# Attention kernel: value products of two steps issued together at every second step, four buffers of exponentials in place of two

## What is computed

```python
B, T, C, H = 8, 1024, 256, 16          # d = C // H = 16
h = layernorm(x) * (1 + ca) + sa
q, k, v = heads(h @ Wq + bq), heads(h @ Wk + bk), heads(h @ Wv + bv)
att = einsum('bhtd,bhsd->bhts', q, k) / sqrt(d)
att = softmax(where(causal, att, -inf), axis=-1)
y = einsum('bhts,bhsd->bhtd', att, v)
x = x + ga * (y.reshape(B, T, C) @ Wp + bp)
```

## Time and profile before

| | us |
|---|---|
| median of 3 runs | 5697.3 |
| lowest and highest run | 5688.06, 5707.4 |
| the profiled execution | 5709.35 |
| span of its profile | 5707.6 |

### The profile page before, as it was taken

One profiled execution on the slowest core, in us unless ns is written; L12 is line 12 of the kernel. 1 busy time (PEld: TensorE's weight loads), 2 busy tenths in 40 slices (PEclk: granted clock), 3 DMA queues, 4 the chain that ended last, 5 costly groups with the idle time before them and its releaser, 6 DMA issues. The chain is left out here.

```text
span 5707.6 us, 95645 instructions
## 1 busy us (share of the span) xinstructions
PE 4571.6 (80%) x31246; PEld 3181.5 (56%) x31246; DVE 3285.3 (58%) x7520; ACT 2605.4 (46%) x5522; POOL 1900.6 (33%) x1482
## 2 busy tenths in 40 slices
PE   2899899899997588887887888848788788787886
PEld 1344444444443466666666666646666666666665
DVE  1555565655553557566575575637557566575564
ACT  0344444444443445455454454535445454454453
POOL 2112212221222334333343343424334343344443
PEclk6787998987887789899899998979899999898988
DMA  5224324423410100000000000020000000000000
GB/s 104 62 42 98 87 42 91 98 42 80 98 31 26 58 16 10 13 13 11 15 12 13 15 10 13 13 59 15 18 21 15 19 17 15 21 15 19 17 17 20
DMA packets 155733, 200.20 MB, mean 35 GB/s; under 512 B 29900, under 2 KB 130728, under 8 KB 155184
## 3 DMA queue, kind: packets, MB, share of 16 engines
q1 hardware_dynamic: 151088, 192.13, 13.8%
q10 hardware_dynamic: 4096, 1.06, 0.1%
HBM read 116.02 MB, written 67.68 MB: 32 GB/s over the span
## 5 line engine op out<-in xcount | busy, mean ns | idle before, releaser
L958 DVE TENSOR_REDUCE a_mx<-a_ring 128x2 f32<-128x1024 f32 (+3 forms) x768 | 728.1, 957 | 439.2 <-PE a_ring L793 293.8
L1477 POOL TENSOR_TENSOR b_e<-b_e,b_share 128x512 f32<-128x512 f32 (+1 forms) x512 | 531.6, 1038 | 1288.6 <-DVE b_share L1905 1288.6
L632 ACT ACTIVATE a_e_t<-a_ring 128x1024 f32<-128x1024 f32 (+3 forms) x768 | 609.3, 810 | 729.0 <-PE a_ring L819 490.2
L1580 ACT ACTIVATE b_e<-b_e,b_bias 128x256 f32<-128x256 f32 (+1 forms) x1024 | 498.7, 488 | 606.5 <-DVE b_bias L1885 605.2
L1683 PE MATMUL b_bank_m<-b_h_t_hi,b_w_hi 128*128 128x256 f32 x1584 | 473.5, 299 | 93.7 <-POOL b_h_t_lo L1483 72.0
L1683 PE MATMUL b_bank_p<-b_wqkv_hi,b_turned_hi 128*128 128x512 f32 x768 | 376.6, 490 | 187.1 <-ACT b_qk L1552 141.2
L788 PE MATMUL a_ring<-a_k_st,a_q_st 48*128 48x512 f32 (+3 forms) x1536 | 370.5, 480 | 125.1 <-ACT a_e_t L632 59.5
L1683 PE MATMUL b_bank_m<-b_h_t_lo,b_w_hi 128*128 128x256 f32 x1584 | 458.9, 290 | 0.0
L1683 PE MATMUL b_bank_m<-b_h_t_hi,b_w_lo 128*128 128x256 f32 x1584 | 458.0, 289 | 0.0
L1885 DVE CUSTOM_DVE_ANT_0 b_e<-b_bank_s,b_mask,b_scale_q 128x256 f32<-128x256 f32 (+1 forms) x1024 | 433.9, 460 | 0.2
L815 PE MATMUL a_ring<-a_q_st,a_k_st 50*128 50x512 f32 (+3 forms) x1536 | 367.1, 475 | 67.6 <-DVE a_qk_p L937 40.3
(11 more groups left out here) (220 smaller groups left out, 11066.7 us busy)
## 6 DMA issues: line engine op xcount, KB each, us to landing
a_q_st<-a_parts_q SPq DMA_DIRECT2D x192, 128.0 KB, 4.4
a_k_st<-a_parts_k SPq DMA_DIRECT2D x192, 128.0 KB, 7.2
b_fl<-f_rows SPq DMA_DIRECT2D x72, 256.0 KB, 4.0
a_parts_q<-a_qk_p SPq DMA_DIRECT2D x16, 1024.0 KB, 9.5
a_parts_k<-a_qk_p SPq DMA_DIRECT2D x16, 1024.0 KB, 4.0
a_xl<-in_L_attn_x SPq DMA_DIRECT2D x9, 1024.0 KB, 9.2
f_rows<-b_fr SPq DMA_DIRECT2D x33, 256.0 KB, 2.3
b_x_l<-x_rows SPq DMA_DIRECT2D x33, 256.0 KB, 3.7
```

Source lines behind the costliest of these rows:

```text
L632: act.activation(e_t[:, step % 2, 2 * pair:2 * pair + 2, 0:cols], slot[:, :].rearrange("p (h t) -> p h t", h=2)[:, :, 0:cols], ACT.Exp).th ...
L958: dve.reduce_max(mx[:, g % 2, :, pair, piece, t:t + 1], slot[:, :].rearrange("p (r c) -> p r c", r=2)[:, :, 0:cols], AX.X)\
L1477: pool.tensor_tensor(weights, weights, share[:, pp, :].unsqueeze(2) .broadcast_to([P, 2, 2 * WIN - lo]), ALU.mult).then_inc(e_done.sem, 1)
L1580: ins = act.activation(weights, weights, ACT.Exp, scale=-1.0, bias=bias[:, pp, hh:hh + 1], accum_out=total[:, pp, hh:hh + 1])
```

## The change

`e_t` gets four buffers (`EBUF = 4`), and ACT waits for the values of four steps before. `meet_values` is no longer called in every step: step n with n even calls it for n - 2 and then n - 1, step 0 for steps 10 and 11 of the group before, and odd steps don't call it. No product, no mask and no reader is added or left out.

```diff
--- before.py
+++ after.py
@@ -221,6 +221,7 @@
 NUNIT = len(UNITS)
 PER_STEP = NUNIT // NSTEP
 UNIT_LEAD = 4
+EBUF = 4
 
 
 def units_at(g, n):
@@ -340,7 +341,7 @@
         q_st = sb("a_q_st", [P, H1 // 2, T], F32R)
         k_st = sb("a_k_st", [P, H1 // 2, T], F32R)
         v_t = sb("a_v_t", [P, TB, H1, VW])
-        e_t = sb("a_e_t", [P, 2, 4, 512])
+        e_t = sb("a_e_t", [P, EBUF, 4, 512])
         w_raw = e_t[:, :, :, :].rearrange("p a b (c n) -> p (a b c) n", n=C)[:, 0:CK * NW, :]\
             .rearrange("p (k w) n -> p k w n", k=CK)
         mx = sb("a_mx", [P, 2, 2, 2, 2, TB])
@@ -627,9 +628,9 @@
                     slot, filled, back, k = slot_of(("s", g, n, pair))
                     act.wait_ge(filled.sem, filled.at(a, k + 1))
                     if pair == 0:
-                        act.wait_ge(values_met.sem, values_met.at(a, step - 1))
+                        act.wait_ge(values_met.sem, values_met.at(a, step - EBUF + 1))
                     cols = 512 * (half + 1) - max(512 * half, P * s)
-                    act.activation(e_t[:, step % 2, 2 * pair:2 * pair + 2, 0:cols],
+                    act.activation(e_t[:, step % EBUF, 2 * pair:2 * pair + 2, 0:cols],
                                    slot[:, :].rearrange("p (h t) -> p h t", h=2)[:, :, 0:cols],
                                    ACT.Exp).then_inc(back.sem, 1)
 
@@ -832,7 +833,7 @@
                         pe.wait_ge(out_read.sem, out_read.at(a, 2 * g + half))
                     for h in range(4):
                         mm = pe.matmul(outp[32 * h:32 * h + VW, lo:512], v_t[:, s, 4 * g + h, :],
-                                       e_t[:, (g * NSTEP + n) % 2, h, 0:512 - lo],
+                                       e_t[:, (g * NSTEP + n) % EBUF, h, 0:512 - lo],
                                        start=(s == 0), stop=(s == 4 * half + 3))
                     mm.then_inc(values_met.sem, 1)
 
@@ -865,9 +866,11 @@
                         scores(g, n, 1, a)
                         for group, k, at in units[1:]:
                             first_pass(group, k, at)
-                        if n > 0:
+                        if n % 2 == 0 and n > 0:
+                            meet_values(g, n - 2, a)
                             meet_values(g, n - 1, a)
-                        elif mode != "lead":
+                        elif n == 0 and mode != "lead":
+                            meet_values((g - 1) % G1, NSTEP - 2, a - (g == 0))
                             meet_values((g - 1) % G1, NSTEP - 1, a - (g == 0))
                         if n == 1 and mode != "lead":
                             turn_output((g - 1) % G1, 1, a - (g == 0), g, a)
@@ -881,6 +884,7 @@
                         if n == 8 and has_maxima(mode, g):
                             turn_maxima(nxt, nxt_a)
                 if mode == "closing":
+                    meet_values(LAST, NSTEP - 2, i)
                     meet_values(LAST, NSTEP - 1, i)
                     turn_output(LAST, 1, i, LAST, i)
                     for at in sorted(AFTER_AT):
```

## The result

The changed kernel takes 5797.2 us, the median of 4 runs (5783.7 to 5814.6), against 5692.7 us for the kernel before beside it (4 runs, 5678.7 to 5707.4). The ratio is **1.0185, with a 95% interval of 1.0147 to 1.0223**: slower, by 104 us. The forecast was 5744 with a range up to 5795. Its sign is right, its size (+47 us) is less than half of what was measured, and the time lies just above the range.

A forecast was written before the change was run, and what follows sets the result against it. PE was taken as the bound by shares, though waiting for ring slots; 48.9 us lost less 17.3 saved gives +31.6, plus 15 for the clock +47, on 5697.3 us makes 5744, range 5695 to 5795.

The forecast's parts named there:

- Part 1: Joining two value products saves 0.09 us for each of 192 pairs, 17 us; ends nothing and 27 us.
- rival C: Readers take ring slots earlier everywhere, only the joining saving of 17 to 27 us remains: 5670 to 5680 us; chance 0.06.
- the free pairs: Pairs at steps 11 to 0, 1 to 2, 5 to 6 and 7 to 8, where nothing was to be lost.
- Part 2: Taking products out of odd steps loses 18.2 us at steps 3 to 4 and 30.7 at 9 to 10, together 48.9.
- So this end is fixed: Steps 9 to 10: ACT's DMAs don't wait for V(8), so moving it costs 0.99 us in each of 31 groups.
- The sum at an unchanged clock: Loss from emptied odd steps less the joining saving, 48.9 - 17.3 = +31.6 us, ends 22 and 49.
- Part 3: Four buffers of exponentials only make the pairing possible, and cost or give nothing.
- Part 4: Clock stays low longer behind step 10, through step 2: +15 us, ends -10 and +40.
- Rival B: Two products in a row hold the clock up, 3.92 us gained per boundary saved: 5666 us; chance 0.08.
- a mean clock in the stretch clearly off 0.86: Sign, in the stretch of the steps, that the forecast is wrong, with the error in its clock term.
- Rival A: Clock much worse: low through step 2 and at more group boundaries, group 0's included, +107 us, 5804; chance 0.17.

The follow-up runs named there:

- the first experiment: The changed kernel with its four buffers kept but no products joined, every step calling its values as before: 5700.3 us, ratio 1.0033 to the kernel before.
- spare ones: The changed kernel plus V(2) computed again in step 3 and V(9) again in step 10, results unread: 5711.7 us, ratio 1.0034 to the kernel before.
- four pairs without a bare product: The changed kernel with pairs only in steps 0, 2, 6 and 8, V(2) and V(8) back in their old steps: 5782.3 us, ratio 1.0190.
- five pairs with one: Two kernels, each the changed kernel with one pair undone: V(2) and V(3) apart, 5722.8 us; V(8) and V(9) apart, 5761.8 us.

## Why the prediction was right and wrong

**Part 1, joining, was too small.** Timeline of PE in the changed kernel, step 8 of group 3, where the passes of a pair can be told apart:

```profile
824.09 1.92 PE L835 MATMUL a_outp<-a_e_t,a_v_t 128*32 128x512 f32 x16
...
825.94 0.28 PE L804 MATMUL a_misc<-a_ident,a_nm 128*32 128x128 f32 x1
```

Two products take 825.94 - 824.09 = 1.85 us, against 2 x 0.99 in rows 3: 0.13 saved, where 0.09 was taken and 0.14 was the upper bound. So the row that stood nearest was the wrong one to go by, and the bound was right. The Trainium skill says in "TensorEngine Tiling (Array Packing)", section "Key Properties", that a change of the tiling mode drains the engine; it was cited beside rival C with the whole 0.14, and this trace agrees. The table adds something that no bound allowed for: the free pairs save 0.13 to 0.35, most of them over 0.2. What the rest beyond 0.14 is was not located.

**Part 2, what is late, was right in its mechanism at both places.** V(2) lost its cover: +0.43 against +0.48. V(8) stands bare behind DMAs that did not move, and PE's wait grew to 1.51 us; near 2 was expected. The loss is +0.87 against +0.90 in three groups. In group 3 it is only +0.29: "So this end is fixed" was read from group 0, and in group 3 the end was PE's own. At the other four boundaries nothing was lost, as said.

**The sum at an unchanged clock was too high.** By the readings above a group comes to +0.3 to +0.7 us in groups 0, 1 and 2 and to -0.3 in group 3. That is about +9 us for 32 groups, not +31.6 (22 to 49). At the full clock the change would be nearly neutral.

**Part 3, the buffers, was right** to within the 0.3% of the first experiment (at most 0.6%).

**Part 4, the clock, is the step that failed.** It was +15, from -10 to +40. The measured share is 64 us, if each of the 196 us more at the lower level holds 0.33, or 78, if it is the rest of the 87. The prediction said "The clock fell behind a step 10, in which PE had idled" and priced only boundaries behind a step 10, between a fall there and V(0). There the lower-level time did not grow at all (272 us before, 257 after). It grew where nothing had been priced: in steps 5 and 6 of groups 2 and 3 (from 24 to 129 us), and inside step 10 ahead of the pair, where two products in a row then run at half speed. The six steps that lost their product leave PE with less to do, and in steps 4 and 10 with a longer wait. The experiments show that the clock follows the work (cut products: 1027 us at the lower level; spare ones: 373). They do not show how much of a fall is due to the wait and how much to the thin step.

The trace of before had a sign of this that the prediction passed over. Of the 37 times that the clock fell in the stretch, 19 begin in steps 10, 11 and 0, but 18 elsewhere: 5 in step 4 of group 0, 3 in step 5 of group 3, and 10 in steps 1, 2, 3 and 6 of group 1. All but two of these 18 lasted under 4 us, so they cost little, but they show that the clock was near falling at other places too. In the changed kernel it fell 69 times, 20 of them in steps 3 and 4 and 24 in step 10 (8 and 11 before). Rival B even took the pair's density as a reason for a gain; a pair raises the density of one step and empties the other.

The text named "a mean clock in the stretch clearly off 0.86" as the sign that would put the error on part 4. It came: 0.80. PE's busy time, which was to fall by some 17 us, rose by 49.

**Rival A** (5804, the clock much worse) is nearest in size, but it is right only in part. It wanted the lower level through step 2, which is seen in group 2 (78.2 of 78.9 us, from 41.6 of 65.7 before). In group 3 the opposite happened (11.1 of 51.4 us, from 45.7 of 67.5). Group 0's boundary did not fall. The Trainium skill's advice in "TensorE: Matmul & The Clock Gate", section "Why this matters for your kernels", is against idle gaps between bursts. In this trace most falls came with waits of 0.6 to 1.5 us ahead, and the cut products show that it can stay down with hardly any.

**What stays open.** Why four pairs without a bare product (5782) lose more clock than five pairs with one (5723 and 5762) is not settled. What a thin step does depends on what stands around it, and no run here isolates that. Where work is taken out of steps, PE's idle share at the full clock rises as well (11.6% before, 12.6% with the four pairs, 12.8% with cut products, 14.0% in the full change), so missing work and waiting stay mixed where the clock falls. Nor is the share of the spare product in step 10 alone, on top of the pairs, known.

## What to carry over

In this kernel, whose granted clock goes back and forth between its levels, PE's work was worth more spread out than joined. Before batching products in such a kernel, read the granted clock by stretch, look at every place where it falls, the short falls too, and ask which steps are left with less. A saving of 0.1 to 0.35 us for each pair was outweighed by two steps that took 10.2 us instead of 6.8. And a short wait of PE for an engine that issues DMAs ahead of its own work is worth removing (here 92 us from issuing two and two instead of four at once); filling it with products that nobody needs gained 65 us, but only while the wait was there.

## What the runs showed of the hardware

- Less work took longer: with the value products of five steps in twelve cut to 32 columns, the stretch held 1027 us at 1.2 GHz instead of 474, and the kernel took 114 us more. Once down, the clock stayed at 1.2 GHz for up to 109 us in which PE waited for 2.8.
- More work took less time: 504 thrown-away matmul records in the stretch took the changed kernel from 5797 to 5712 us.
- Two column-tiled products in a row save nearly the whole fixed part of the first one's end, 0.13 of 0.99 us.
- Four small DMAs issued by ACT hold its compute for 2.43 us, two for 1.15.
- The same order of instructions had 474 us at 1.2 GHz in one execution and 361 in another, with the stretch 34 us apart.
